# Norm statistics made ahead inside the attention, and four banks for its last outputs

## What is computed

```python
x = x + _L0_xattn_ref(ctx_1024, _layernorm(x, axis=-1), ...)   # a state-space scan
x = x + _L0_ffn_ref(_layernorm(x, axis=-1), ...)               # mixture of experts, top 8 of 64
x = x + _L1_xattn_ref(_layernorm(x, axis=-1), ctx_1024, ...)   # attention, 16 heads of 128
x = x + _L1_ffn_ref(_layernorm(x, axis=-1), w1, w2)            # feed-forward, 512 -> 2048 -> 512

def _layernorm(x, axis=-1, eps=1e-05):
    m = jnp.mean(x, axis=axis, keepdims=True)
    v = jnp.var(x, axis=axis, keepdims=True)
    return (x - m) / jnp.sqrt(v + eps)
```

## Time and profile before

| | us |
|---|---|
| three runs | 3130.51, 3134.58, 3138.97 |
| median | 3134.58 |
| the profiled execution | 3123.35 |
| its span | 3121.9 |
| TensorE busy | 2486.2 (80%) |
| VectorE busy | 2022.6 (65%) |
| ScalarE busy | 1250.3 (40%) |
| GpSimd busy | 1585.2 (51%) |
| attention (its units and last outputs) | about 1923 to 2912 of the span |
| statistics of the feed-forward's norm | 2912 to 2928 |
| feed-forward | 2928 to 3109 |

### The profile page before, as it was taken

The page is one execution under the profiler, slowest core; times in us unless marked ns, Lnnn a source line. Parts: engine busy times, 40 slices in busy tenths (PEclk is TensorE's granted clock), DMA queues, the critical chain, the costliest instruction groups (busy, mean ns, idle before and its releaser), DMA issues. The chain is left out here.

```text
span 3121.9 us, 42803 instructions
## 1 busy us (share of the span) xinstructions
PE 2486.2 (80%) x11156; PEld 1739.9 (56%) x11174; DVE 2022.6 (65%) x3178; ACT 1250.3 (40%) x2245; POOL 1585.2 (51%) x1291
## 2 busy tenths in 40 slices
PE   7825555555979489999999974989989999999586
PEld 3301222214767367667777753768777777888343
DVE  3579999997869334564444446675676666555596
ACT  3424344443345232221121212545545555555275
POOL 2446565563047666665666726654664664444010
PEclk9869999997989799999999986999999999999898
DMA  2016666662369798887777755434443543332101
GB/s 84 9 41 217 224 211 223 214 216 98 142 240 341 262 335 274 299 298 238 248 243 249 239 168 162 139 129 142 141 134 112 169 138 111 124 109 68 54 0 54
DMA packets 260694, 538.30 MB, mean 172 GB/s; under 512 B 24400, under 2 KB 90064, under 8 KB 259808
## 3 DMA queue, kind: packets, MB, share of 16 engines
q1 hardware_dynamic: 207296, 347.98, 32.6%
q0 software_dynamic: 44032, 167.80, 16.3%
q10 hardware_dynamic: 9248, 21.11, 2.0%
HBM read 328.14 MB, written 208.67 MB: 172 GB/s over the span
## 5 line engine op out<-in xcount | busy, mean ns | idle before, releaser
L523 PE MATMUL ps_y<-c_state,ident 128*128 128x512 f32 x512 | 268.7, 651 | 205.2 <-DVE c_state L475 204.9
L448 POOL TENSOR_TENSOR b_u<-du,bc 128x1024 f32<-128x1024 f32 x128 | 301.3, 2354 | 212.0 <-DVE c_state L475 176.5
L1711 ACT ACTIVATE prob<-ps_s,neg,q_rs 128x512 f32<-128x512 f32 x256 | 196.9, 774 | 320.5 <-DVE neg L1883 320.5
L1230 PE MATMUL ps_o<-w_dn,hid_t 96*128 x632 | 309.1, 612 | 0.0
L523 PEld LDWEIGHTS ps_y<-c_state,ident 128*128 128x128 f32 x512 | 91.4, 198 | 382.0 <-DVE c_state L475 313.6
L467 DVE TENSOR_TENSOR_SCAN state<-ps_decay,b_u 128x1024 f32<-128x1024 f32 x128 | 293.1, 2290 | 16.4 <-issue 9.0
L1795 POOL TENSOR_SCALAR prob<-prob,rden 128x512 f32<-128x512 f32 x256 | 174.6, 692 | 248.1 <-DVE rden L1891 248.1
L1266 ACT ACTIVATE silu_g<-ps_gu 128x192 f32<-128x192 f32 x159 | 52.5, 330 | 544.2 <-PE ps_gu L1211 544.2
L419 ACT ACTIVATE ps_decay<-delta,a_neg 128x511 f32 x256 | 165.9, 681 | 223.0 <-DVE state L467 222.7
L1211 PE MATMUL ps_gu<-w_gu_high,rows_t_high 128*128 (+1 forms) x636 | 229.2, 360 | 10.8 <-POOL w_gu_low L1095 9.5
L1095 POOL TENSOR_TENSOR w_gu_low<-raw_gu,w_gu_high 128x1536 fp32r<-128x1536 f32 x64 | 222.7, 3480 | 12.0 <-POOL w_gu_high L1093 12.0
(11 more groups left out here) (302 smaller groups left out, 6058.1 us busy)
## 6 DMA issues: line engine op xcount, KB each, us to landing
rows_dram<-zeros SPq DMA_DIRECT2D x15, 3584.0 KB, 14.3
raw_gu<-in_gate_up POOLq DMA_DIRECT2D x64, 768.0 KB, 5.4
rows<-rows_dram SPq DMA_DIRECT2D x160, 256.0 KB, 3.8
y_dram<-y SPq DMA_DIRECT2D x158, 256.0 KB, 3.4
bc<-bc_dram SPq DMA_DIRECT2D x64, 512.0 KB, 5.8
w_q<-wq_dram SPq DMA_DIRECT2D x64, 512.0 KB, 3.7
w_o<-wo_dram SPq DMA_DIRECT2D x16, 2048.0 KB, 9.1
w_dn<-in_down POOLq DMA_DIRECT2D x64, 384.0 KB, 5.7
```

The costliest lines, as they stand in the source:

```text
L448: pool.tensor_tensor(out=b_u[:, ec % 2, :, :], in0=m.du[:, ds1(b * EC + ec), :].broadcast_to([P, G, SEQ]), in1=bc[:, par, 0, :, :], op=ALU ...
L523: mm = pe.matmul(ps_y[ec][:, :], c.ident[:, :], c_state[:, ec % 2, g, :], start=False, stop=False)
L1230: mm = pe.matmul(ps_o[par][:, :], hid_t[par][:, k, :], w_dn[:, ds1(slot), k, :].rearrange("p a f -> p (a f)"), start=k == 0, stop=k == 1)
L1711: act.activation(prob[:, qt, :], ps_s[qt % 2][:, :], ACT.Exp, scale=q_rs[:, k % 2, qt:qt + 1], bias=neg[:, qt:qt + 1], accum_out=den[:, qt ...
```

## The change

`norm_statistics` gets a parameter `first`, and the call ahead of the feed-forward passes 12: it handles tiles 12 to 15 alone. The statistics of batches 0 to 2 are made in the attention, during the batch that follows, by a function `ended_stats` at the end of VectorE's unit and `ended_root` at the end of GpSimd's: one tile's bn_stats and bn_aggr in each of units 4 to 7, the addition of eps in unit 8, the power in unit 9, nbias in unit 10. The last four outputs go to ps_yo, ps_s0, ps_s1 and ps_p0 in place of ps_yo alone.

```diff
-def norm_statistics(nc, c, tag, loads=()):
+def norm_statistics(nc, c, tag, loads=(), first=0):
...
-            with dve.Fori(0, NT) as t:
+            with dve.Fori(first, NT) as t:
...
-            dve.wait_ge(stats_made, NT)
-            for t in range(NT):
+            dve.wait_ge(stats_made, NT - first)
+            for t in range(first, NT):
                 aggr = dve.bn_aggr(bn2[:, t, :], bn6[:, t, :])
...
+        last_banks = [ps_y, ps_s[0], ps_s[1], ps_p[0]]
...
-            def output(pp, grp, t):
+            def output(pp, grp, t, bank=ps_y):
...
-                wait(pe, y_added, g * ST + t)
+                wait(pe, y_added, g * ST + t if bank is ps_y else 0)
                 wait(pe, t_low, tokens_turned[0])
-                product(ps_y[:, :], [(both(o_t, lambda x: x[:, grp, h, t * P:(t + 1) * P]),
+                product(bank[:, :], [(both(o_t, lambda x: x[:, grp, h, t * P:(t + 1) * P]),
...
             for t in range(ST):
-                output(NPP - 1, 1, t)
+                output(NPP - 1, 1, t, last_banks[t])
...
+            def ended_root(pp, k):
+                b, k = (pp * U + k) // NH - 1, (pp * U + k) % NH - HG
+                if b >= 0 and k == ST + 1:
+                    waits(e_eps, b + 1)
+                    pool.tensor_tensor(out=c.rstd[:, b * ST:(b + 1) * ST], in0=f_vare[:, :], in1=c.power[:, 0:ST],
+                                       op=ALU.pow).then_inc(e_rooted, 1)
...
                 gather(pp, k, 2)
+                ended_root(pp, k)
...
+            def ended_stats(pp, k):
+
+                b, k = (pp * U + k) // NH - 1, (pp * U + k) % NH - HG
+                if b < 0:
+                    return
+                if 0 <= k < ST:
+                    n = b * ST + k
+                    wait(dve, e_rooted, b)
+                    dve.bn_stats(f_bn6[:, k, :], c.X[:, n, :]).then_inc(e_stats, 1)
+                    dve.wait_ge(e_stats, n + 1)
+                    dve.bn_aggr(f_bn2[:, k, :], f_bn6[:, k, :]).then_inc(e_aggregated, 1)
+                if k == ST:
+                    dve.wait_ge(e_aggregated, (b + 1) * ST)
+                    dve.tensor_scalar(out=f_vare[:, :], in0=f_bn2[:, :, 1], scalar1=EPS, scalar2=None, op0=ALU.add)\
+                        .then_inc(e_eps, 1)
+                if k == ST + 2:
+                    dve.wait_ge(e_rooted, b + 1)
+                    t = slice(b * ST, (b + 1) * ST)
+                    dve.scalar_tensor_tensor(out=c.nbias[:, t], in0=f_bn2[:, :, 0], scalar=-1.0, in1=c.rstd[:, t],
+                                             op0=ALU.mult, op1=ALU.mult)
...
                 token_stats(pp, k)
                 token_norm(pp, k)
+                ended_stats(pp, k)
...
-                add(NPP - 1, 1, t)
+                add(NPP - 1, 1, t, last_banks[t])
...
-            norm_statistics(nc, c, "n3", loads)
+            norm_statistics(nc, c, "n3", loads, first=(BATCH - 1) * ST)
```

More of the change, by code:

```diff
@@ L149, in _ @@
             dve.wait_ge(aggregated, 1)
-            dve.tensor_scalar(out=vare[:, 0:NT], in0=bn2[:, 0:NT, 1], scalar1=EPS, scalar2=None,
+            dve.tensor_scalar(out=vare[:, first:NT], in0=bn2[:, first:NT, 1], scalar1=EPS, scalar2=None,
                               op0=ALU.add).then_inc(eps_added, 1)
             dve.wait_ge(rooted, 1)
-            dve.scalar_tensor_tensor(out=c.nbias[:, 0:NT], in0=bn2[:, 0:NT, 0], scalar=-1.0, in1=c.rstd[:, 0:NT],
+            dve.scalar_tensor_tensor(out=c.nbias[:, first:NT], in0=bn2[:, first:NT, 0], scalar=-1.0, in1=c.rstd[:, first:NT],
                                      op0=ALU.mult, op1=ALU.mult)
@@ L159, in _ @@
             pool.wait_ge(eps_added, 1)
-            pool.tensor_tensor(out=c.rstd[:, 0:NT], in0=vare[:, 0:NT], in1=c.power[:, 0:NT],
+            pool.tensor_tensor(out=c.rstd[:, first:NT], in0=vare[:, first:NT], in1=c.power[:, first:NT],
                                op=ALU.pow).then_inc(rooted, 1)
@@ L1458, in attention @@
         f_rooted, f_biased, f_normed = p.sem("f_rooted"), p.sem("f_biased"), p.sem("f_normed")
+        e_stats, e_aggregated, e_eps, e_rooted = (p.sem(x) for x in ("e_stats", "e_aggregated", "e_eps", "e_rooted"))
         f_turned, f_high, f_low = p.sem("f_turned"), p.sem("f_high"), p.sem("f_low")
@@ L1901, in out_part, with add @@
                 low(o_t[1][:, grp, h, :], ps_o[:, :], o_t[0][:, grp, h, :], o_high, pp * U + k + 1, o_low)
-            def add(pp, grp, t):
+            def add(pp, grp, t, bank=ps_y):
                 g, b = pp * 2 + grp, pp // 2
@@ L1906, in add @@
                 x = c.X[:, ds1(b * ST + t), :].rearrange("p a l -> p (a l)")
-                dve.tensor_tensor(out=x, in0=ps_y[:, :], in1=x, op=ALU.add).then_inc(y_added, 1)
+                dve.tensor_tensor(out=x, in0=bank[:, :], in1=x, op=ALU.add).then_inc(y_added, 1)
             def before(pp, k):
```

## The result

| | before | changed |
|---|---|---|
| median, 15 runs each, us | 3132.05 | 3123.30 |
| lowest and highest, us | 3122.58, 3140.16 | 3114.11, 3134.69 |
| span of the profiled execution, us | 3121.9 | 3115.6 |

The ratio is 0.9969, with a 95% interval of 0.9957 to 0.9980: by it the kernel is 9.7 us faster, between 6.3 and 13.5 (the two medians lie 8.75 us apart). The forecast was 2.5 us faster. The sign was right, and the measured time lies in the range, but the gain is nearly four times the forecast, and even the interval's lower end, 6.3 us, is more than twice the 2.5.

A forecast was written before the change was run, and what follows sets the result against it. TensorE was taken to pace the attention, with VectorE close behind, and the seam to be unoverlapped. 13.1 us saved less 10.5 spent, rounded to 2.5, gave a median of 3132.1 us from 3134.58; range 3122 to 3140.

The forecast's parts named there:

- The seam: Between attention and feed-forward: four banks save 3.2 us, fewer statistics and a shorter power 9.9 us, together 13.1 us.
- The load of w1q: At the feed-forward's start: its landing moves 3.2 us ahead, to 2917.8, and VectorE still comes last by 0.8 us.
- Batch 3's pairs: Units 4 to 7 of batch 3: each 0.81 us pair, less 0.40 us slack, costs 0.41 us; 1.6 us in all.
- nbias in its unit 10: Batch 3, unit 10: four-column nbias stands 1.29 us beside k_t_low, less 0.40 us slack, costing 0.9 us.
- The power in unit 9: Batches 1 and 2: GpSimd's added power makes the token norm's nbias stand 1.02 us longer, costing 2.0 us.
- Rival B: Unit 9's power is free, nbias getting the port between GpSimd's instructions: cost 8.5 us, gain 4.6 us, 3130.0 us; chance 0.10.
- Units 4 to 7 of batches 1 and 2: Pairs at these units' ends: 0.58 us each in units 4 and 7 (2.3 us), 0.81 in 5 and 6 (3.2 us).
- Eps in unit 8: One small tensor_scalar at unit 8's end: 0.1 us in batches 1 and 2, none in 3; 0.2 us.
- rival C: Longer waits in units 5 and 6 of batches 1 and 2 bring low-clock stretches: 7 us slower, 3141.7 us; chance 0.07.
- Rival A: VectorE's added work in the attention is covered by waits, only unit 9's power costs: gain 11.1 us, 3123.5 us; chance 0.18.
- D: At the seam, w1q's landing stays at 2921.0, so 2.4 us of the gain are lost: 3134.5 us; chance 0.05.
- E: At the seam, the four banks bring nothing because TensorE waits for something else; 3.2 us missing, 3135.3 us; chance 0.05.

The follow-up runs named there:

- seam alone: Changed kernel without the calls of ended_stats and ended_root, so nothing is added inside the attention; ratio 0.9963 (0.9949 to 0.9976).
- eps: Changed kernel with the addition of eps in unit 8 as four one-column instructions instead of one of four columns; unit 8 of batch 3 took 14.04 us.
- slack-place: Changed kernel with all added VectorE work moved ahead of the low part of the third transposed probability tile, same units; one execution took 3128.8 us.
- late-units: Changed kernel with VectorE's added work earlier in the unit, pairs in units 11 to 14, eps and power in 14, nbias in 15; ratio 0.9947.
- banks-alone: Kernel before with only the four banks for the last outputs, all 16 tiles' statistics still after the attention; ratio 0.9999 (0.9983 to 1.0016).
- pairs-alone: Changed kernel with the twelve bn_stats and bn_aggr pairs but without eps, power and nbias of batches 0 to 2; batch 3's units 4 to 7 took 14.43 to 14.45 us.
- combined: Changed kernel with pairs in units 11 to 14, plus a useless GpSimd power between last gather and k_t_low in token-norm units; ratio 0.9930, 3108.66 us.
- memset kernel: Kernel before plus a useless four-column GpSimd memset between the gather and k_t_low; single execution, nbias 0.15 us in unit 9 of batch 1.

## Why the prediction was right and wrong

**The seam** was right: 13.1 us forecast, 13.1 with the seam alone, 12.6 in the changed kernel. Every term stood within about 0.1 us: the adds at 2.72 us (2.76 forecast), twelve fewer bn_stats (7.1), 0.8 us for the bn_aggr (0.88), a power of 1.02 us. The missing 0.5 us is the idle time of 1.98 us ahead of the first bn_stats; it was 1.98 in the changed, eps, slack-place and late-units kernels and 1.54 in the banks-alone, seam-alone, pairs-alone and combined ones. I don't know what decides it. The load of w1q stayed hidden, with 0.4 us of margin.

**Batch 3's pairs** were right within 0.01 us: 0.41 us forecast, 0.40 measured, four times. nbias in its unit 10 was right too (0.9 forecast, 0.77; the instruction took 1.25 us, 1.29 forecast).

**The power in unit 9** was the step that failed, and by sign. I wrote that nbias would stand 1.02 us longer, since the power would come between. It cost +2.0 in the sum and gave 0.95 us back in each of two batches: 3.9 us wrong. I had read the row of 2.07 us as VectorE standing through whatever GpSimd does in a row. What it showed was narrower: nbias stands when k_t_low is what follows the issue. What I had drawn from the Trainium skill, "SBUF — State Buffer", section "Who interferes with whom", that the power would cost nothing "or even less", was the better guide, though nbias slipped in ahead of the power and not of k_t_low. Rival B, which priced it at zero, should have had the gain as well. Neither its sign (2.07 us) nor the forecast's (3.1) came.

**Units 4 to 7 of batches 1 and 2** were 5.5 us in the sum. They came out at 1.7 and 1.8 us, 3.5 together. Of this, unit 4 was over-priced. Where the clock doesn't fall in it, it takes 16.37 us before (batch 2) and 16.58 changed (batch 1), which is 0.2 us and not 0.58. That is just what the neg behind it gives back: it takes 0.16 us in the changed kernel, where the earlier trace rows has 0.75, and 0.81-0.59 = 0.22. I had scaled from another row instead. And a loss in unit 6 is partly given back in unit 7. That the units behind have no reserve holds for batch 3 alone.

**Eps in unit 8** was priced at 0.2 us and none in batch 3. It cost 0.81 us there and 1.0 in each of the others: 2.8. The step that failed is "one small tensor_scalar": the row beside it, 0.15 us, was of one column, and four columns wait for GpSimd.

In sum: 10.5 us forecast in the attention, 6.5 to 7.5 measured, with one term of 3.9 and one of 2.0 too high and one of 2.6 too low. That leaves a net of -12.6+7 = -5.6, just short of the measured -6.3 to -13.5. What makes up the rest stays open. The feed-forward was 2.4 us shorter in the changed kernel's trace, but that is not shown to be the change's doing. In the seven profiles with the short seam it took 186.9 to 190.05 us, 188.6 in the mean; in the five with the long one 186.9 to 190.2, 189.3 in the mean. It goes roughly with TensorE's granted clock in that stretch: 0.92 before (190.2 us), 0.93 with the seam alone (190.05 us), 0.94 changed (187.8 us), and 0.95 in both executions of 186.9 us, of which one, the memset kernel, has the old seam.

**The clock** (rival C) did fall more often, without the price. Its sign came, new stretches at the low clock: one more in each of batches 1 and 2, and in each of them one that stands in unit 6, behind the wait that the pair had made longer (2.19 us for 1.41), and none in unit 5. C priced such a stretch at 2.4 us. With the pair's own cost in it, units 6 and 7 together came out only 1.1 us longer than undisturbed ones, less than the 1.39 that the sum gave to the two pairs alone. The slack-place kernel, whose clock didn't fall in batch 2 at all, has the same 34.6 us there. So C did not turn the result, and no run shows a price of these stretches beside the pairs' own.

**Rival A** would have looked right by the time alone: it said 3123.5 us, and 3123.30 was measured. The traces refute it, since 6.5 to 7.5 us are paid in the attention. Rivals D and E fell with the rows above.

**Luck** had a part. Two errors were too high (3.9 and 2.0 us) and one too low (2.6), and the measured median lies 1.3 us above the lower end of a range that the spread of the runs had made 18 us wide. The median of before itself moved from 3134.58 to 3132.05 us with twelve more runs.

## What to carry to other kernels

A step that is moved costs what the wait at its new place leaves over, not its duration: the same statistics, with eps, power and nbias, cost 6.5 to 7.5 us at the end of units 4 to 10. A few instructions earlier in the same units batch 3, where VectorE had idled 0.96 us there, took them for nothing, and in units 11 to 15 all three batches did. Before such a step is priced, its exact shape has to be found among the rows, down to the number of columns. And in an order written out by hand an instruction can be waiting for the one that its neighbour engine will start next; look at what ends together with it.

## What the runs showed of the hardware

- A VectorE tensor_scalar of 128x4 fp32 in SBUF waited for GpSimd's 128x512 subtraction (1.08 us), and four of 128x1 didn't (0.33 us together). Where no such subtraction ran, the 128x4 one took 0.16 to 0.17 us.
- VectorE's scalar_tensor_tensor of 128x1, two inputs in SBUF, stood 2.07 us through an indirect DMA's issue and the GpSimd subtraction behind it. With a GpSimd power, subtraction or memset between the two it took 0.15 to 0.19 us in units 3, 6 and 9, in 22 of 24 cases of the three kernels with one spare instruction (unit 3 of batch 0 is left out, where it took 0.15 us before as well). So it isn't the issue itself that holds VectorE up, and the hold begins before the subtraction's own start in the record (2331.64 in the earlier trace rows, with VectorE waiting since 2330.90).
- A GpSimd power of 128x4 takes 1.02 to 1.08 us, a subtraction of the same size 0.21 and a memset 0.12.
- TensorE's granted clock fell to its lower level in the last value product in some executions of kernels that do the same there (0.50 between 2890 and 2892), which made it 1.6 us longer, and not in others.
- Behind a wait of 2.17 to 2.19 us in unit 6 the granted clock fell to 0.50 for about 3.4 us in six of six cases; behind the wait of 1.41 us in the kernel before it did not. It also fell without so long a wait, as from 2249.5 in the kernel before, where TensorE had waited 0.63 us.
